# Rescaling the running softmax sums on ScalarE instead of VectorE in six edge passes

## The reference

```python
e = jax.nn.leaky_relu(el[src] + er[dst], 0.2)
m = jax.ops.segment_max(e, dst, num_segments=n)
ex = jnp.exp(e - m[dst])
denom = jax.ops.segment_sum(ex, dst, num_segments=n)
alpha = ex / denom[dst]
h_gat = jax.ops.segment_sum(alpha[:, :, None] * z[src], dst, num_segments=n)
```

## Time and profile before

| | |
|---|---|
| median of three runs | 13878.64 us (13873.74 to 13880.02) |
| profiled execution | 13875.03 us, its span 13873.3 us |
| VectorE busy | 10723.6 us (77%) |
| TensorE busy | 8685.8 us (63%) |
| GpSimd busy | 6951.8 us (50%) |
| ScalarE busy | 2809.5 us (20%) |
| relational passes | 1831 to 2970, 3497 to 4632, 5095 to 6229 us |
| edge-attention pass | 8403 to 9532 us |
| convolution passes | 9859 to 11722, 11900 to 13762 us |

### The profile page before, as it was taken

The page is one execution under the profiler, slowest core; times in us unless marked ns, Lnnn a source line. Parts: engine busy times, 40 slices in busy tenths (PEclk is TensorE's granted clock), DMA queues, the critical chain, the costliest instruction groups (busy, mean ns, idle before and its releaser), DMA issues. The chain is left out here.

```text
span 13873.3 us, 209115 instructions
## 1 busy us (share of the span) xinstructions
PE 8685.8 (63%) x52858; PEld 7028.6 (51%) x52859; DVE 10723.6 (77%) x16335; ACT 2809.5 (20%) x4518; POOL 6951.8 (50%) x7719
## 2 busy tenths in 40 slices
PE   4663577767778678773566636773666665666664
PEld 3552255553566446553555524552555554555554
DVE  7666479964899559985888867998677877677777
ACT  0110222223222232220444412221000000000000
POOL 3774057730777227760777706773344443344442
PEclk8555788878788788886888856665788888788887
DMA  4335754437444464451555612222233333333333
GB/s 179 113 112 131 266 165 105 104 53 295 112 105 104 113 260 106 105 93 28 141 147 145 141 23 51 54 54 23 86 96 92 93 95 69 95 93 93 95 93 65
DMA packets 720170, 1523.50 MB, mean 110 GB/s; under 512 B 364796, under 2 KB 416585, under 8 KB 680627
## 3 DMA queue, kind: packets, MB, share of 16 engines
q0 software_dynamic: 306624, 795.04, 24.1%
q1 hardware_dynamic: 413427, 727.07, 15.4%
HBM read 1050.48 MB, written 471.10 MB: 110 GB/s over the span
## 5 line engine op out<-in xcount | busy, mean ns | idle before, releaser
L967 POOL DMA_INDIRECT h<-table,edges_ring x3984 | 3785.5, 950 | 1291.0 <-issue 1161.1
L1146 PE MATMUL bank<-h,edges_onehot 128*128 128x260 f32 (+1 forms) x7968 | 2150.6, 431 | 717.6 <-DVE acc L1307 396.4
L1146 PEld LDWEIGHTS bank<-h,edges_onehot 128*128 128x128 f32 x7968 | 1693.8, 263 | 1130.2 <-DVE acc L1307 458.7
L1241 DVE TENSOR_TENSOR_SCAN bank<-edges_fresh,edges_top,bank 4x1024 f32<-4x1024 bf16 x660 | 1542.0, 2336 | 426.8 <-PE bank L1121 426.8
L967 POOL DMA_INDIRECT edges_rows<-table,edges_ring x1512 | 1492.3, 987 | 465.0 <-issue 415.7
L1121 PE MATMUL bank<-ident,edges_score 128*4 128x128 f32 x5280 | 1017.2, 358 | 953.1 <-DVE edges_score L1271 797.3
L1248 DVE TENSOR_TENSOR_SCAN edges_top<-edges_fresh,bank 4x1024 f32<-4x1024 bf16 x660 | 1497.0, 2268 | 0.2
L956 POOL COPY edges_ring<-src_idx 128x8 uint32 (+1 forms) x440 | 90.7, 207 | 2759.4 <-PE bank L1146 1356.4
L1121 PEld LDWEIGHTS bank<-ident,edges_score 128*4 128x4 f32 x5280 | 495.9, 104 | 1266.9 <-DVE edges_score L1271 841.9
L1307 DVE TENSOR_TENSOR acc<-acc,bank 128x260 f32 (+1 forms) x2640 | 919.8, 348 | 206.1 <-DVE acc L1297 59.8
L2010 POOL DMA_INDIRECT rec<-dst,slots x782 | 797.1, 1019 | 433.6 <-issue 433.2
(11 more groups left out here) (345 smaller groups left out, 16680.7 us busy)
## 6 DMA issues: line engine op xcount, KB each, us to landing
table<-x SPq DMA_DIRECT2D x154, 1040.0 KB, 7.9
edge_score<-edge_feat SPq DMA_DIRECT2D x220, 512.0 KB, 3.7
table<-h SPq DMA_DIRECT2D x77, 1040.0 KB, 7.9
table<-source_typed_rows SPq DMA_DIRECT2D x63, 1040.0 KB, 8.1
h<-table,edges_ring POOLq DMA_INDIRECT x3984
edge_feat<-edge_score SPq DMA_DIRECT2D x110, 512.0 KB, 3.0
dst_row<-dst_rows SPq DMA_DIRECT2D x71, 704.0 KB, 4.2
buf<-rec SPq DMA_DIRECT2D x44, 840.0 KB, 5.2
```

The costliest lines, as they stand in the source:

```text
L967: pool.indirect_dma_start(out=rows[s % R][:, j, :], out_offset=None, in_=table, in_offset=bass.IndirectOffsetOnAxis(ap=ring[:, s * ST + j: ...
L1146: ins = pe.matmul(sum_b[k % 3], onehot[s][:, j, :], rows[s][:, j, A0:W], start=j == k * GT, stop=j == (k + 1) * GT - 1)
L1241: v.tensor_tensor_scan(score_b[0:HEADS, :], fresh[s][:, 0:SLOTS_SB], score_b[0:HEADS, :], top[1 - s][:, SLOTS_SB - 1:SLOTS_SB], ALU.add, A ...
```

## The change

The factor and the scaling leave VectorE. ScalarE makes the factor with one activation (Identity, with `hot` as a scale and `cold` as a bias per partition) right after `rate`, and multiplies the four heads' sums by four copies with a scale per partition, at the end of the step of `m`, which is one step earlier than VectorE did it. For that ScalarE loads one bin number itself. `factor` gets two buffers and a semaphore `factor_made`.

```diff
-        factor = p.buffer("factor", (P, HEADS))
+        factor = [p.buffer(f"factor{s}", (P, HEADS)) for s in range(2)]
...
             @block.scalar
             def _(act):
+                def scale_sums(m, first_bin):
+                    u, s = number(m), m[1] % 2
+                    az = g.acc[:, bass.ds(first_bin, 1), D:D + ZW].rearrange("p b c -> p (b c)")
+                    act.wait_ge(factor_made, u + 1)
+                    hold(act, sums_taken, GPS * u)
+                    for head in range(HEADS):
+                        part = az[:, head * HZ:(head + 1) * HZ]
+                        ins = act.activation(part, part, ACT.Copy, scale=factor[s][:, head:head + 1])
+                    ins.then_inc(sums_scaled, 1)
...
                         act.wait_ge(top_turned, u + 1)
-                        hold(act, sums_scaled, u - 1)
                         act.activation(rate[s % 2][:, :], fall_b, ACT.Exp).then_inc(rate_made, 1)
+                        act.wait_ge(rate_made, u + 1)
+                        act.activation(factor[s % 2][:, :], rate[s % 2][:, :], ACT.Identity,
+                                       bias=g.cold[:, bass.ds(u, 1)], scale=g.hot[:, bass.ds(u, 1)]).then_inc(factor_made, 1)
                         act.wait_ge(arg_made, u + 1)
...
                     if n and conv is None:
                         narrow_ahead(after(n))
+                    if m:
+                        scale_sums(m, load_bin(act, g, number(m), 0))
...
-                def scale_sums(o, c, bins):
-                    u, s = number(o), o[1] % 2
-                    az = g.acc[:, bass.ds(bins[0], 1), D:D + ZW].rearrange("p b (h z) -> p (b h) z", h=HEADS)
-                    v.wait_ge(rate_made, u + 1)
-                    c.link(v.scalar_tensor_tensor(factor[:, :], rate[s][:, :], g.hot[:, bass.ds(u, 1)],
-                                                  g.cold[:, bass.ds(u, 1)].to_broadcast([P, HEADS]), ALU.mult, ALU.add))
-                    hold(v, sums_taken, GPS * u)
-                    v.tensor_tensor(az, az, factor[:, :].unsqueeze(2).to_broadcast([P, HEADS, HZ]), ALU.mult
-                                    ).then_inc(sums_scaled, 1)
...
                         bins = load_bins(v, g, number(o))
-                        scale_sums(o, c, bins)
                         add_sums(o, 0, bins)
```

More of the change, by code:

```diff
@@ L1010, in attention_edges @@
         rate = [p.buffer(f"rate{s}", (P, HEADS)) for s in range(2)]
-        factor = p.buffer("factor", (P, HEADS))
+        factor = [p.buffer(f"factor{s}", (P, HEADS)) for s in range(2)]
         gathered, seen = g.gathered, p.gathers_before()
         (ring_kept, onehot_made, onehot_flipped, flipped_kept, dst_spread, score_made, score_turned, rising_made, top_made,
-         fall_made, top_turned, arg_made, weight_made, weight_kept, rate_made, sums_scaled, rows_weighted, sums_made, sums_taken,
+         fall_made, top_turned, arg_made, weight_made, weight_kept, rate_made, factor_made, sums_scaled, rows_weighted, sums_made, sums_taken,
          chain, cleared) = (p.semaphore(n) for n in (
              "ring_kept", "onehot_made", "onehot_flipped", "flipped_kept", "dst_spread", "score_made", "score_turned",
-             "rising_made", "top_made", "fall_made", "top_turned", "arg_made", "weight_made", "weight_kept", "rate_made", "sums_scaled",
+             "rising_made", "top_made", "fall_made", "top_turned", "arg_made", "weight_made", "weight_kept", "rate_made", "factor_made", "sums_scaled",
              "rows_weighted", "sums_made", "sums_taken", "chain", "cleared"))
@@ L1214, in _ @@
                 LB = 0
-                LC = 1
+                LC = 0
                 def onehot_ahead(n):
```

## The result

| | before | after |
|---|---|---|
| median of seven runs | 13880.76 us (13873.74 to 13886.71) | 13832.59 us (13826.0 to 13839.47) |
| span of the profiled execution | 13873.3 us | 13832.7 us |
| ratio | | 0.9965 [0.9954, 0.9977] |
| four passes without convolution | 1139, 1135, 1134, 1129 us | 1124, 1124, 1123, 1121 us |
| two convolution passes | 1863, 1862 us | 1863, 1861 us |

The change saves 48 us, 0.35%. The forecast was 13714 us with a range from 13655 to 13800, and the result lies above it. The passes show where it went wrong. These are the stretches of the changed kernel, to be read beside the earlier trace rows: length, busy PE, PEld, DVE, ACT, POOL, granted clock, DMA share, GB/s.

The account below looks back on a forecast made before the run. GpSimd's issue, with VectorE, was taken to bound the four passes, the VectorE-TensorE chain the convolution. 13875.03 less 125 (convolution) and 40 (other passes) gave 13710, or 13714 us as a median; range 13655 to 13800.

Parts of the forecast that it names:

- the price of the convolution: Two convolution passes: 220 steps each win a mean 0.57 us, 125 us in all, bounds 64 and 172.
- the rooms: Convolution steps: slack before TensorE's second half and VectorE's taking it up, 0.86 us in one step, 0.29 in another.
- all of 0.78 us: Rival, convolution passes: the clock rises and every step wins the full 0.78 us; total 13662 us, chance 0.12.
- The rooms shrink as they are used: Rival: 0.29 us per convolution step becomes the rule and GpSimd's stalls stay; 64 + 10 us, 13805 us, chance 0.15.
- The four other passes: Passes without convolution: GpSimd's 10.10 us becomes the bound and their lateness goes; 40 us gained, bounds 0 and 45.
- GpSimd's own pace: Passes without convolution: eight gathers and the index copy take 10.10 us, 0.25 us under the step seen.
- the free pace of the earlier trace: First relational pass: at 10.10 us each, the 108th superblock would start at 2897.5, where it started at 2913.39.
- its stalls of 1.85 us: GpSimd's issue, passes without convolution: 1.85 us instead of 0.30 once every 12 superblocks, expected to go.
- ScalarE's price: ScalarE's added work: four scaling copies 1.07 us, bounds 0.97 and 1.3; the factor 0.33 us, bounds 0.17 and 0.6.
- The order in a relational step: Relational step: scaling starts at the narrowing's end, the add about 1.1 us after it; fits, or costs VectorE 0.1 us.
- The signs for the convolution: Profile of convolution passes: first add about 3.0 us after the scan's start, more TensorE idle time ended by ScalarE's copy.
- The passes 60 us shorter: Profile sign: each of the two convolution passes some 60 us shorter.

Follow-up runs that it names:

- e2_conv_only: Changed kernel with ScalarE scaling only in the two convolution passes, old code in the other four: 13882.72 us, ratio 0.9998 to the kernel before.
- e12: Changed kernel plus 14 unused TensorE products before the turned scores and 5 before the second half, in convolution steps: 13451.82 us, ratio 0.9688.
- e17: Kernel before plus 14, 5 and 4 unused TensorE products, the 4 ahead of the one-hot flip, in convolution steps: 13650.32 us, ratio 0.983.
- e10: Changed kernel with VectorE loading the bins ahead of the first scan in the convolution passes: 13832.23 us, ratio 0.9964.
- e1: Changed kernel with ScalarE scaling only in the four passes without convolution, old code in the convolution: 13837.51 us, ratio 0.9965 to the kernel before.
- e11: Kernel before plus 14 unused TensorE products before the turned scores and 5 before the second half, in convolution steps: 13859.73 us, ratio 0.9984.
- e18: Changed kernel plus only the 14 unused TensorE products in the long pause of convolution steps: 13589.89 us, ratio 0.9787 to the kernel before.
- e19: Changed kernel plus only the 5 unused TensorE products in the short pause of convolution steps: 13692.39 us, ratio 0.9861 to the kernel before.
- e4: Changed kernel plus 22 unused TensorE products before the turned scores and 8 before the second half, in convolution steps: 13729.48 us, ratio 0.9887.
- e5_early_loads: Changed kernel with bins loaded ahead of the scan in convolution passes, run where the kernel before took 16035.98 us: ratio 1.0235.

## Why the prediction was wrong

**The step that failed** is the price of the convolution: "Their mean, capped at 0.78, is 0.57 us. So 220 x 0.57 = 125 us for the two passes". It measured 1 us in the profiles and 4 us in `e2_conv_only`, within that run's uncertainty. The subtraction itself can be repeated: over all steps of the two passes the rooms give 0.57 and 0.53 us. But it takes rooms between rows of one trace as if TensorE's durations stayed. They didn't: the products of a pass took 84 us more and the share at 1.2 GHz rose from 0.26 to 0.34. The sentence "the clock shows no sign of following so small a change" is the wrong one behind it. I had used it against the rival "all of 0.78 us", which had the clock rise as the pauses shrink. It fell. None of the rivals had that. The rival "The rooms shrink as they are used" had a part of what happened, the waits for ScalarE's copy, but it left 64 us of gain to the convolution.

**The mechanism, and how far it is shown.** An experiment shows that the gain depends on the clock: with TensorE held at 2.4 GHz the same edit gives 145 us (`e12` against `e17`), and with the clock free it gives 1 to 4. That the 40 further falls took it is read from the rows, where TensorE's products take 84 us more; no run adds falls alone. With the clock free, a second cut of 0.9 us a step gives nothing either (`e10`), there at an unchanged clock, where the waits point to TensorE's own way round as the longer one. The Trainium skill, TensorE: Matmul & The Clock Gate, Part 1, says that an idle TensorE gets half its clock and a busy one the whole of it. The filler agrees (0.83 without, 0.88 and 0.93 with one pause filled, 1.00 with both). By that rule alone the changed kernel, whose TensorE waits 607 us a pass instead of 685, should have had more of the clock, and it got less. Why the falls multiplied stays open.

**What held, and what was a little off.**
- The four other passes: 45 us for 40. GpSimd became the bound: in the middle of the first pass (80 steps) a step takes 10.09 us, for 10.33 before, and GpSimd's own pace is 10.10. Its 108th superblock starts where the free pace of the earlier trace rows puts it, 2897.5 us, and its stalls of 1.85 us are gone: its longest wait in its own issue is 0.3 us in all four passes, where it was 1.7 to 1.9. VectorE waits for gathers all through, as expected, 73 times in the first pass. That GpSimd would never wait for TensorE did not come true: it still does, 19 times and 6.9 us in all.

```profile
2897.39 0.98 POOL L967 DMA_INDIRECT edges_rows<-table,edges_ring  x1 [0.16 <-issue]
```

```profile
POOL h L967 <- issue: 183.9, 640, 0.3
...
POOL h L967 <- PE bank L1146: 4.9, 12, 1.7
```

```profile
DVE edges_spread L1290 <- DMA h<-table,edges_ring: 55.5, 57, 4.0
```

- ScalarE's price: four copies in 0.96 us for 1.07, the factor 0.39 us for 0.33. The estimate from the Trainium skill, ScalarE: Activation LUTs, What ACT_TABLE_LOAD costs, was 0.945 us for the copies, and the trace agrees. No engine is seen to wait for the scaling in the first relational and the first convolution pass, so that page's advice (Rules for kernel authors) to give a plain multiply to VectorE did not matter. The groups of ScalarE (busy us, mean ns, idle before):

```profile
L1182 ACT ACTIVATE acc<-acc,edges_factor x2640 | 627.5, 309 | 92.2 <-issue 91.3 <-DVE acc L1311 0.9
...
L1207 ACT ACTIVATE edges_factor<-edges_rate,cold,hot 128x4 f32<-128x4 f32 x660 | 256.4, 389 | 92.8
```

- The order in a relational step: the scaling right behind the narrowing, the add without a wait. The narrowing ends at 2297.90, the add starts 1.18 us later, where 1.91 had been and 1.1 was forecast.

```profile
2296.84 1.06 ACT L1188 ACTIVATE edges_narrow_onehot<-edges_onehot 128x1024 bf16<-128x1024 f32 x1 [2.40 <-DVE edges_onehot L946]
2297.80 0.95 ACT L1182 ACTIVATE acc<-acc,edges_factor  x4
...
2299.08 0.42 DVE L1311 TENSOR_TENSOR acc<-acc,bank 128x260 f32 x1
```

- The signs for the convolution: the first add came 3.17 us after the scan's start for 3.0, and TensorE waits more for ScalarE's copy, as forecast. The passes 60 us shorter did not come.
- A convolution step took 17.07 us and not 16.9: the 110 scans of a pass bound 109 steps. No term of the sum hung on it.

Some 5 us of the 46 that the six passes gave are missing in the span (40.6 us). The stretch between the third relational pass and the edge-attention pass is 14 us longer in the changed kernel's profile (2190 us for 2176), and the other stretches between passes are 9 us shorter. In the profiles of eight other runs that stretch takes 2181 to 2192 us, with the old code and with the new, so its length says nothing of the change.

## What to carry to other kernels

Where a chain runs to and fro between TensorE and another engine and the mean granted clock is between its levels, as here (0.87 and 0.83), TensorE's durations are not constants: price a cut of the other engine's work only at a clock that is held, and look at the granted clock of the stretch first. Filling TensorE's pauses with products of no use took 381 us (2.8%) off the changed kernel without touching its work. They must fit the pauses (22 and 8 of them left 13729 us where 14 and 5 gave 13452) and reach all of them (the kernel before won 21 us with two pauses filled and 237 with three), and they must be tried on more than one chip, since on some the kernel with them was slower. Of the cuts tried here the best kernel is the changed one with 14 and 5 added products and early loads, 13412 us.

## What the runs showed that I had not expected

- The two convolution passes took 1861 to 1863 us in four kernels (the changed one, `e1`, `e2`, `e10`), as before, although the first add came up to 1.5 us earlier after its scan. Single steps differ much, 15.4 to 18.3 us in the changed kernel and 15.9 to 17.9 in `e10`, but the first pass's mean step is 17.05 to 17.07 us in all five. So it is in the middle of `e11` (80 steps) too, at another clock. Steps and falls repeat in a pattern, in `e10` from three steps to three, with 50.9 to 51.5 us for three. It looks as if the steps had locked to the rhythm of the clock's own changes, so that a small cut of the work shifts the falls and not the mean. No run tests that. With no falls the step is 16.0 us (`e17`) and 15.3 us (`e12`), and with one pause filled it leaves 17.07 as well (15.96 in `e18`, 16.4 in `e19`).
- Where all was slower (once on the very chip that had run `e1` to `e4` at their usual times), TensorE's records end well before its work does. In `e5_early_loads`:

```profile
12613.61 0.49 PE L1111 MATMUL bank<-edges_w_e,edge_score 128*128 128x128 f32 x2
...
12617.87 0.69 DVE L1246 TENSOR_TENSOR h<-h,bank 128x512 f32<-128x512 f32 x1 [4.83 <-DMA table<-x]
12618.05 0.34 SPq L1058 DMA_DIRECT2D edge_score<-edge_feat  x1
```

  VectorE and SyncE both wait for that half and go on at about 12617.9, 3.8 us after the last record of it. The releaser in brackets is a guess of the profile; in the kernel's code both wait for the semaphore that the half's last product raises. Either TensorE stood still in between or its signal came late. What held it no record says. Nor is the clock the whole of it: it was granted at 0.75 in that pass, where the changed kernel had 0.83.
